# A graph-attention layer on one core: layer-2 output with tokens on partitions, DMA-transposed in f16 halves for the FFN

## The reference

```python
h = relu(layernorm(x))
x = x + deg * (h @ Wi.T + b0) + adj @ (h @ Wj.T)
h = relu(layernorm(x))
heads = [elu(softmax(mask(leaky(f1 + f2.T))) @ (h @ W[m])) for m in range(4)]
v = concat(heads) @ W_out
out = elu(softmax(mask(leaky(g1 + g2.T))) @ v)
y = relu(out @ w1 + b1) @ w2 + b2 + out
x = x + layernorm(y) * gamma + beta
```

## Time and profile before

| | us |
|---|---|
| median of 3 runs | 1723.54 |
| lowest, highest | 1720.91, 1724.05 |
| profiled execution, first to last instruction | 1722.6 |
| busy PE, DVE, ACT, POOL in it | 1584.4, 1452.3, 1382.1, 1004.7 |

### The profile page before, as it was taken

How to read it: one execution, slowest core, us unless ns; L and a number is a source line. 1 busy time by engine, 2 the same in 40 slices (tenths; PEclk the granted TensorE clock), 3 DMA queues, 4 the chain that set the end, 5 groups by cost and what they waited for, 6 DMA issues and landing times.

```text
span 1722.6 us, 36184 instructions
## 1 busy us (share of the span) xinstructions
PE 1584.4 (92%) x13119; PEld 1319.3 (77%) x13120; DVE 1452.3 (84%) x2520; ACT 1382.1 (80%) x1858; POOL 1004.7 (58%) x1425
## 2 busy tenths in 40 slices
PE   5548999999999999999999999999999999999965
PEld 3336878788787887788887887888777888888854
DVE  5877699879998899979999799988999798898583
ACT  4177499879988799878997799878997799999660
POOL 4064367447575566656575566656666475675271
PEclk9769999999999999999999999999999999999988
DMA  8266499749986698678977699868976698798572
GB/s 262 57 147 115 94 190 162 120 95 189 174 151 117 123 187 164 118 122 160 189 141 117 113 184 178 137 98 152 190 156 112 104 172 172 129 133 147 101 118 36
DMA packets 780882, 242.45 MB, mean 141 GB/s; under 512 B 746368, under 2 KB 774016, under 8 KB 780576
## 3 DMA queue, kind: packets, MB, share of 16 engines
q1 hardware_dynamic: 771744, 231.70, 72.1%
q0 software_dynamic: 8960, 8.42, 4.3%
HBM read 38.54 MB, written 16.94 MB: 32 GB/s over the span
## 4 chain that ended last, share of the span: by engine, by line
PE 49%; DVE 18%; ACT 13%; issue 10%; DMA 5%; POOL 3%; SPq 1%; DVEq 0%; ACTq 0%; POOLq 0%
PE ps L129 11%; PE ps L1260 7%; PE ps L1261 7%; PE ps L1266 7%; DVE p_lo L1041 5%; PE ps L138 5%; PE ps L1280 4%; PE ps L1293 3%; ACT p_hi L925 3%; ACT xr L912 3%; DVE xr L1034 3%; PE ps L1341 2%; DMA cat<-f_rows 2%; ACT xr L918 2%; DVE ht_lo L1066 2%
## 5 line engine op out<-in xcount | busy, mean ns | idle before, releaser
L1260 PE MATMUL ps<-pt_hi,hv_hi 128*128 128x256 f16 x2048 | 463.8, 274 | 26.4 <-DMA pt_hi<-p_hi 26.4
L1261 PE MATMUL ps<-pt_hi,hv_lo 128*128 128x256 f16 x2048 | 463.7, 274 | 0.0
L1041 DVE SCALAR_TENSOR_TENSOR p_lo<-xr,rden,p_hi 128x1024 f16<-128x1024 f32 x320 | 409.6, 1280 | 30.4 <-ACT p_hi L925 30.4
L925 ACT ACTIVATE p_hi<-xr,rden 128x1024 f16<-128x1024 f32 x320 | 365.4, 1142 | 32.8 <-POOL rden L849 32.8
L847 POOL TENSOR_SCALAR den<-sums 128x1 f32<-128x1 f32 x320 | 156.4, 489 | 363.2 <-ACT xr L918 361.2
L918 ACT ACTIVATE xr<-xr,shift 128x1024 f32<-128x1024 f32 x320 | 365.5, 1142 | 2.4 <-POOL shift L862 2.4
L1034 DVE CUSTOM_DVE_ANT_0 xr<-cat,mask_add 128x1024 f32<-128x1024 f32 x256 | 311.2, 1217 | 7.5 <-DMA cat<-f_rows 7.5
L912 ACT ACTIVATE xr<-xr,f1h 128x1024 f32<-128x1024 f32 x256 | 292.6, 1143 | 5.5 <-DVE mx L1034 5.5
L849 POOL TENSOR_TENSOR rden<-den,minus_one 128x1 f32<-128x1 f32 x320 | 268.3, 838 | 26.7
L860 POOL TENSOR_SCALAR zt<-mx,f1h 128x1 f32<-128x1 f32 x256 | 197.6, 772 | 120.0 <-DVE mx L1034 117.1
L1266 PE MATMUL ps<-pt_lo,hv_hi 128*128 128x256 f16 x2048 | 266.3, 273 | 0.9 <-DMA pt_lo<-p_lo 0.9
(11 more groups left out here) (192 smaller groups left out, 3193.3 us busy)
## 6 DMA issues: line engine op xcount, KB each, us to landing
cat<-f_rows SPq DMA_DIRECT2D x32, 512.0 KB, 4.6
out<-xx SPq DMA_DIRECT2D x32, 256.0 KB, 2.4
xx<-in_x SPq DMA_DIRECT2D x28, 256.0 KB, 3.3
...
pt_hi<-p_hi SPq DMA_TRANSPOSE x320, 3.3
pt_lo<-p_lo SPq DMA_TRANSPOSE x320, 3.3
...
```

Source lines behind the costliest of these rows:

```text
L925: nc.scalar.activation(p_hi[:, k % P_SLOTS, :], xr[:, k % X_SLOTS, :], ACT.Copy, scale=rden[:, k % 8:k % 8 + 1]).then_inc(hi_done, 1)
L1041: nc.vector.scalar_tensor_tensor(p_lo[:, k % P_SLOTS, :], xr[:, k % X_SLOTS, :], rden[:, k % 8:k % 8 + 1], p_hi[:, k % P_SLOTS, :], ALU.mu ...
L1260: nc.tensor.matmul(to, vh, hi, start=t == 0, stop=False)
L1261: nc.tensor.matmul(to, vl, hi, start=False, stop=False)
```

## The change

Layer 2's attend swaps its operands: the transposed attention rows become the stationary operand and the values the moving one, one unit after the other. The result has 128 tokens on partitions and 256 features in a row. Each unit waits for its own high half and then for its own low half. ELU writes it to fin in that layout. ACT (o2_high) and DVE (o2_low) split it into f16 parts, SP transposes both by DMA into hs_hi and hs_lo (turn_o2), and ff1 is made in three f16 passes from there, with w1 split in the setup and its scale taken back in hidden. ff2 no longer adds the input: y_out adds fin, which now has the right layout, and b2 comes as a bf16 product of 65 rows (pick, b2_rows). The tables shift, GAP becomes 8, and turn_h0 waits until ff1 has read hs.

```diff
+            def turn_o2(j):
...
+                c = count2(j)
+                cols = slice(i // 4 * N + i % 4 * F, i // 4 * N + (i % 4 + 2) * F)
+                for whole, part, ready in ((hs_hi, o2_hi[:, c % 2, :], o2hi_done), (hs_lo, o2_lo[:, :], o2lo_done)):
+                    sp.wait_ge(ready, c + 1)
+                    sp.dma_start_transpose(whole[:, cols].rearrange("p (t i) -> p t i", i=P), part).then_inc(o2_T[c % 2], DMA)
...
+            def o2_high(j):
+                c = count2(j)
+                act.wait_ge(elu_done, j + 1)
+                if c >= 2:
+                    act.wait_ge(o2_T[c % 2], c // 2 * 2 * DMA)
+                nc.scalar.activation(o2_hi[:, c % 2, :], o2_of(j), ACT.Copy, scale=scale(S_O2)).then_inc(o2hi_done, 1)
...
+            def o2_low(j):
+                c = count2(j)
+                dve.wait_ge(o2hi_done, c + 1)
+                if c:
+                    dve.wait_ge(o2_T[(c - 1) % 2], (c + 1) // 2 * 2 * DMA)
+                nc.vector.scalar_tensor_tensor(o2_lo[:, :], o2_of(j), scale(S_O2), o2_hi[:, c % 2, :], ALU.mult, ALU.subtract).then_inc(o2lo_done, 1)
...
+                if layer == 2:
+                    for u in range(2):
+                        to = psA[:, (j % 2) * 512 + u * F:(j % 2) * 512 + (u + 1) * F]
+                        pe.wait_ge(hi_T[slot + u], turn)
+                        for t in range(T):
+                            hi = pt_hi[:, slot + u, t * P:(t + 1) * P]
+                            nc.tensor.matmul(to, hi, vals[0][:, t, :], start=t == 0, stop=False)
+                            nc.tensor.matmul(to, hi, vals[1][:, t, :], start=False, stop=False)
+                        pe.wait_ge(lo_T[slot + u], turn)
+                        for t in range(T):
+                            last = nc.tensor.matmul(to, pt_lo[:, slot + u, t * P:(t + 1) * P], vals[0][:, t, :], start=False, stop=t == T - 1)
+                    last.then_inc(mm_done, 1)
+                    return
...
-                pe.wait_ge(elu_done, first2[p] // 2 + 2 * i + 2)
+                for slot in range(2):
+                    pe.wait_ge(o2_T[slot], (2 * p + i + 1) * 2 * DMA)
+                hi, lo = half_T(i)
                 for m in range(KF):
-                    last = product(to[:, m * 512:(m + 1) * 512], [(w1_sb[:, k, m * P:(m + 1) * P], o2T_of(p, i)[:, k, :]) for k in range(KF)])
+                    last = product(to[:, m * 512:(m + 1) * 512].rearrange("p (t n) -> p t n", n=P),
+                                   [(w[:, k, m * P:(m + 1) * P], h[:, k, :, :]) for k in range(KF) for h, w in ((hi, w1_hi), (hi, w1_lo), (lo, w1_hi))])
...
                     for k in range(KF):
                         nc.tensor.matmul(to[:, t * F:(t + 1) * F], ff_half[:, k * 512 + t * P:k * 512 + (t + 1) * P], w2_sb[:, k, :], start=k == 0, stop=False)
-                    for k in range(KF):
-                        last = nc.tensor.matmul(to[:, t * F + k * P:t * F + (k + 1) * P], o2T_of(p, i)[:, k, tok], ident[:, :], start=False, stop=k == KF - 1)
+                    last = nc.tensor.matmul(to[:, t * F:(t + 1) * F], pick[:, :], b2_rows[:, :], start=False, stop=True)
...
-        GAP = 6
+        GAP = 8
...
-        CLOSING = dict(ff1_0=-1, ff2_0=2, ff1_1=4, ff2_1=6, hidden_0=1, hidden_1=5, y_0=4, y_1=9, save_f2o=-22, load_f2o=-16)
-        LAST = dict(ff1_0=3, ff2_0=3, ff1_1=5, ff2_1=7, hidden_0=2, hidden_1=5, y_0=4, y_1=8, save_f2o=-13, load_f2o=-12)
+        CLOSING = dict(ff1_0=2, ff2_0=4, ff1_1=6, ff2_1=8, hidden_0=3, hidden_1=7, y_0=5, y_1=9, save_f2o=-22, load_f2o=-16)
+        LAST = dict(ff1_0=2, ff2_0=3, ff1_1=5, ff2_1=7, hidden_0=2, hidden_1=5, y_0=4, y_1=8, save_f2o=-15, load_f2o=-14)
```

More of the change, by code:

```diff
@@ L158, in scores_T @@
                 for t in range(T):
-                    last = nc.tensor.transpose(to[:, t * NF:(t + 1) * NF], rows[:, t * P:(t + 1) * P], ident[0:NF, 0:NF])
+                    last = nc.tensor.transpose(to[:, t * NF:(t + 1) * NF], rows[:, t * P:(t + 1) * P], ident8[0:NF, 0:NF])
                 return last
@@ L367, in _ @@
                     nc.scalar.activation(wo_hi[:, :, F:V], wao[:, :, :], ACT.Copy, scale=scale(S_WAO)).then_inc(whi_done, 1)
+                    nc.scalar.activation(w1_hi[:, :, :], w1_sb[:, :, :], ACT.Copy, scale=scale(S_W1)).then_inc(whi_done, 1)
                 @block.vector
@@ L576, in _ @@
                     product(psA[:, 0:F], [(ones[:, :], sqo[:, k * F:(k + 1) * F]) for k in range(KH)])
+                    pe.wait_ge(sq_done, 3)
+                    product(psA[:, F:2 * F], [(ones[:, :], sqw[:, k * F:(k + 1) * F]) for k in range(KF)])
                     pe.wait_ge(sqa_done, 1)
@@ L618, in build @@
         fin = sb("fin", [P, 3, N], F32)
+        o2_hi = sb("o2_hi", [P, 2, 2 * F], F16)
+        o2_lo = sb("o2_lo", [P, 2 * F], F16)
         ff_half = fin[:, 2, :]
@@ L641, in build @@
         mjhi_done, m_done, x1_half = sem("mjhi_done"), sem("m_done"), sem("x1_half")
-        o2T_done, ff_done, y_done = sem("o2T_done"), sem("ff_done"), sem("y_done")
+        o2hi_done, o2lo_done, ff_done, y_done = sem("o2hi_done"), sem("o2lo_done"), sem("ff_done"), sem("y_done")
+        o2_T = [sem(f"o2_T_{i}") for i in range(2)]
         K = B * (U1 + U2)
-        GAP = 6
+        GAP = 8
         first1 = [0, U1] + [2 * U1 + U2 + (U1 + U2) * i for i in range(B - 2)]
@@ L740, in y_of, with o2_of, count2, half_T @@
             return fin[:, i, :] if b < B - 1 else cat[:, i, :]
-        def o2T_of(b, i):
-            return y_of(b, i).rearrange("p (k n) -> p k n", k=KF)
+        def o2_of(j):
+            layer, b, i = kinds[2 * j]
+            return y_of(b, i // 4)[:, i % 4 * F:(i % 4 + 2) * F]
+        def count2(j):
+            layer, b, i = kinds[2 * j]
+            return (U2 * b + i) // 2
+        def half_T(i):
+            return [whole[:, i * N:(i + 1) * N].rearrange("p (t k n) -> p k t n", k=KF, n=P) for whole in (hs_hi, hs_lo)]
         block = ctx.enter_context(nc.Block())
@@ L783, in turn_h0 @@
                     sp.wait_ge(bank_full[which], seq + 1)
+                if s >= 3:
+                    which, seq = bank(f"ff1_{i}", s - 3)
+                    sp.wait_ge(bank_full[which], seq + 1)
                 half_of = slice(i * N, (i + 1) * N)
@@ L798, in turn_h1 @@
                                            part[s % 2][:, tiles, :].rearrange("p t f -> p (t f)")).then_inc(h1T_in, DMA)
+            def turn_o2(j):
+                layer, b, i = kinds[2 * j]
+                if i % 4 == 0:
+                    which, seq = bank("rows", min(b + 2, B - 1))
+                    if b:
+                        seq = max(seq, bank(f"ff1_{i // 4}", b - 1)[1])
+                    sp.wait_ge(bank_full[which], seq + 1)
+                c = count2(j)
[3 more added lines that the diff above has]
+                    sp.dma_start_transpose(whole[:, cols].rearrange("p (t i) -> p t i", i=P), part).then_inc(o2_T[c % 2], DMA)
             for n in range(START, STOP):
@@ L809, in _ @@
                     sp.dma_start_transpose(pt_lo[:, slot, :].rearrange("p (t i) -> p t i", t=T), p_lo[:, row, :]).then_inc(lo_T[slot], DMA)
+                j = pair_at(n - O2_LOW)
+                if j is not None and kinds[2 * j][0] == 2:
+                    turn_o2(j)
                 for s in range(B):
@@ L980, in hidden @@
                 for m in range(KF):
-                    last = nc.scalar.activation(ff_half[:, m * 512:(m + 1) * 512], general(which)[:, m * 512:(m + 1) * 512], ACT.Relu, bias=b1_col[:, m:m + 1])
+                    last = nc.scalar.activation(ff_half[:, m * 512:(m + 1) * 512], general(which)[:, m * 512:(m + 1) * 512], ACT.Relu, bias=b1_col[:, m:m + 1],
+                                                scale=scale(S_FF1))
                 last.then_inc(ff_done, 1)
@@ L1003, in _ @@
                     ht_high(j)
+                j = pair_at(n - O2_HIGH)
+                if j is not None and kinds[2 * j][0] == 2:
+                    o2_high(j)
                 for s in range(B):
@@ L1139, in y_out @@
                 y = y_of(p, i).rearrange("p (t f) -> p t f", f=F)
-                nc.vector.tensor_tensor(y, general(which)[:, :].rearrange("p (t f) -> p t f", f=F), b2_bc[:, :].unsqueeze(1).to_broadcast([P, half, F]), ALU.add).then_inc(y_done, 1)
+                nc.vector.tensor_tensor(y, general(which)[:, :].rearrange("p (t f) -> p t f", f=F), y, ALU.add).then_inc(y_done, 1)
                 hold(dve, "dve", y_done, 2 * p + i + 1)
@@ L1187, in _ @@
                     ht_low(j)
+                j = pair_at(n - O2_LOW)
+                if j is not None and kinds[2 * j][0] == 2:
+                    o2_low(j)
                 for s in range(B):
```

72 lines of the change are left out of this document (47 added, 25 removed).

## The result

| | before | after |
|---|---|---|
| median, 4 runs each (us) | 1723.80 | 1780.50 |
| lowest, highest | 1720.91, 1724.97 | 1777.01, 1785.12 |
| profiled execution, first to last instruction | 1722.6 | 1774.9 |

A forecast was written before the change was run, and what follows sets the result against it. PE and DVE were taken to share the bound, DVE pacing attention rows and PE the rest. Terms 0.3 + 0 - 0.5 - 2.0 - 4.4 = -6.6 took the span from 1722.6 to 1716.0, forecast 1717 us, range 1700 to 1729.

The forecast's parts named there:

- Prologue +0.3: Setup: DVE's added work meets a wait for the score rows, costing 0.3 us, or 1.5 without that cover.
- Five periods 0: Steady 200 us periods, one per sample: PE's savings and DVE's delays nearly cancel, -0.1 us each, taken as 0.
- The waits of the m products: Steady period: m0-m1 and m2-m3 each share an interval, giving two 1 us waits per sample, one of them new.
- Sixth FFN -0.5: FFN at 1450 to 1500 us, followed by layer-1 pairs alone: 0.5 us gained, between -3 and +2.
- The gap -2.0: Gap before the last sample: its attention starts earlier, but ACT and transposes pace it; 2.0 us gained, -4 to 0.
- The end -4.4: Last sample's plain closing chain: both FFN halves shorten by 2.2 us, 4.4 in all; second half's transpose just fits.
- Rival 3: Added ACT and DVE work and SP's wait become the bound: 2.6 us lost per period, 1733 us, chance 0.18.
- Rival 4: New idle stretch each period drops PE to half clock, 1.7 us of work each time: 1727 us, chance 0.10.
- Rival 2: Layer 2's new product order lifts the row pace, 2 us more gained per period: 1707 us, chance 0.20.
- Rival 1: All of PE's relief arrives, 4.4 us gained in each of five periods: 1693 us, chance 0.12.
- The idle stretch of 3 to 5 us before E: Sign: PE idles before each first layer-1 pair after layer 2, awaiting its transposes, and the chain enters PE there.
- DVE's idle time at the neighbour products: Sign: DVE's idle time in the stretch where PE does the neighbour products falls from 10 to some 6 us.

The follow-up runs named there:

- b_steady: Kernel before with only the changed STEADY table (m products, mj_high, mj_low and turn_h0 one step later): 1740.01 us, ratio 1.0083.
- b_closing: Kernel before with only the changed CLOSING table (FFN products, ReLU and y of samples 0 to 6 one to three steps later): 1755.10 us, ratio 1.0178.
- b_tables: Kernel before with all of the change's tables and GAP = 8, but the old computation: 1770.36 us, ratio 1.0267.
- a_mlow: Changed kernel with one order swapped on DVE, mj_low ahead of gain within a step: 1772.90 us, ratio 1.0269 to the kernel before.
- a_noturn: Changed kernel without the 64 transposes of o2 and their waits, splits still made: 1775.38 us, ratio 1.0282 to the kernel before.
- a_nosplit: Changed kernel without o2_high, o2_low and the 64 transposes, so without the FFN's real input: 1759.27 us, ratio 1.0187 to the kernel before.
- b_attend: Kernel before with only layer 2's new operand order in attend, FFN input thus in the wrong layout: 1722.03 us, ratio 0.9979.

## Why the prediction was wrong, point by point

- *Prologue +0.3*: right within the scatter of the traces, 0.0 at pair 0. But 4.0 us were lost by pair 24, most of it from the moved m products of the third sample (from pair 0 to 24 b_steady loses 3.5, b_closing 0.3). I had no term for that.
- *Five periods 0, bounds -4.4 and +3*: this is the step that failed. It measured +8.4, +7.4, +5.8, +6.6 and +5.6. The sum let the chain enter PE's stretch at E and counted all FFN work from there on as one total, 13.0 instead of 13.9. These two lengths came true. But PE's chain begins at F: E started 0.5 us earlier after B and not 1.7, and F waited 3.31 us for the ELU of D, so that F stands at the same distance from B as before (35.6, 35.3). Up to F less work gains nothing, and only what stands behind F counts. What I left out is where the moved products went: I counted what an FFN product costs, and not which waits it had filled before, nor what it stands ahead of now. ff2_0, once between E and F, and everything behind it now stand a pair later, in the stretch that was full. There FFN work is 10.4 us instead of 8.7: 1.7 us more, with 3.2 more idle time and 1.7 of clock 6.6 of the 7.1. b_tables, which moves the steps alone, loses 23.5 of the 33.8 us of the five periods.
- *The waits of the m products at 1 us each*: wrong at m1, 2.73 and 0.87 elsewhere. m0 and m1 now share an interval, and DVE's gain stands ahead of m_low. a_mlow takes 3.0 us off the period shown by that alone, 2.3 on average.
- *Sixth FFN -0.5*: +7.0 (pair 124 to 148). b_closing, the FFN's steps alone, loses 6.9 there. *The gap -2.0*: +11.7. I had looked at the relief and not at what the later ReLU is queued behind; b_closing shows it without any transpose (pair 157 at +34.4, pair 155 at +21.7), and transposes that land late come on top (a_noturn loses 8.5 there, the changed kernel 11.7). *The end -4.4*: -2.6. The products are shorter as forecast (2.6 and 3.9 us), but PE waits 1.70 us at 1741.83 for the transpose of the low part of the first half. I had looked at the second half's alone, which fit; for the first I had no term. Without transposes (a_noturn) the end is 4.4 shorter.
- *Rival 3, the production side*, had the right sign and the wrong cause. DVE does take over the chain behind F, but by the order of its work; the splits cost 1.4 to 1.8 us of a period, the transposes nothing (a_nosplit, a_noturn), and the period lost 7 us, not 2.6. *Rival 4, the clock*, happened, though at other places than ahead of E: 0.95 from B to F, where it costs nothing that shows, and 0.61 behind m1, 1.7 us, in four of the five periods. The Trainium skill, page "TensorE: Matmul & The Clock Gate" (section "HAM oscillation"), says that a loop with one long gap per turn is throttled anew in every turn. Each of the five periods has at least one fall, which agrees; behind m1 alone one of five came without (945.22). *Rival 2* did not come: b_attend gains 3.4 us in all, none of it shown to lie in the periods. *Rival 1* did not come.

Of the announced signs, the product lengths came true, and the period above 201 us was the one named as making the forecast wrong. The idle stretch of 3 to 5 us before E did not come: PE stood still 2.37 before D, 0.61 before E and 3.31 before F, each time for an ELU and not for E's transposes. DVE's idle time at the neighbour products stayed at 10 (24.87 busy of 35.20 us from 765.5), where I had announced 6.
